# Third cross attention: the exponentials of two key chunks are added on GpSimd before the denominators are summed on TensorE

## The chip, the cores and the metric

One core of a Trainium2 chip runs the whole program in one launch. The metric is the device time of one execution in microseconds (us). The time of a kernel is the median of several executions.

## The reference, cut to what matters

The program is eight layers on x of shape (8, 128, 256): four pairs of a gated cross attention and a gated feed-forward layer. The change is in the third cross attention (L2). With x normalised as the query and the context as key and value, both (batch, 128, 256) read as D = 128 by T = 256:

```python
qh = q.reshape(B, 8, 16, 256)          # 8 heads of 16 rows, 256 queries
kh, vh = k.reshape(B, 8, 16, 256), v.reshape(B, 8, 16, 256)
qn, kn = _l2norm(qh, axis=-2), _l2norm(kh, axis=-2)
sm = softmax(5.0 * einsum('bhdq,bhdk->bhqk', qn, kn), axis=-1)
out = einsum('bhqk,bhdk->bhdq', sm, vh)
x = x + tanh(g_xattn[2]) * out
```

The softmax is computed as exponentials of the scores (no maximum is taken off, since they lie within 5), a product of the exponentials with the values, a sum of the exponentials over the 256 keys (the denominator), and a division at the end.

## The kernel before, in words

The program is written for each engine by hand: each engine has one queue in which its instructions stand in order, and waits on semaphores order them against other engines. The layers run one after another. In this layer (`xa2_*`) the names are these:

- A **step** u = 0 to 15 is one batch b = u // 2 and one half k = u % 2 of its heads: four heads, numbered g = 0 to 3. All is f32. The 256 keys come in two **chunks** kc of 128 (DC = 2).
- `scores(u)` (L1392, matmuls at L1403) makes the scores of four heads, transposed: keys on partitions, 256 queries in the free direction. Four heads sit in four row groups of the array (32 rows each). The results are in two pairs of PSUM banks: pair 2u for heads 0 and 1, pair 2u + 1 for heads 2 and 3. It waits for the masked keys (`km_ready`), the normalised query of the batch (`q2_ready`, once per batch) and for a pair of banks to be free (`p2_ready`).
- ScalarE (L1446) exponentiates one pair at a time, 128x1024, into a slot of `PT2`. PT2 has four slots, which is two steps; a slot holds [head of the pair, chunk, query]. It waits for `v2_done` of the step two before.
- `values(u)` (L1408) waits until both pairs are exponentiated. Then for each chunk it has four passes for the values (L1418, one per head, into four column groups of 32, so they run side by side) and four passes with ones as weights (L1422) that sum the exponentials over the keys of that chunk into `total`. Both accumulate in one PSUM bank over chunks and both halves of the heads. The four denominator passes of the last chunk each count up `v2_done`. `values(2b)` waits also for `o2_read`, count b - 1, which VectorE gives when it has divided batch b - 2 (there are two such banks).
- TensorE's order is scores(0), then scores(u + 1), values(u) in turn, and values(15).
- VectorE (`xa2_dve`, L1457) first does for all eight batches: clamp of the query norms (L1345, 128x256 in SBUF, in place), reciprocal (L1347), multiplication of the query by it (L1462, two SBUF operands), which gives `q2_ready`. After the eighth it goes on to `norm_dve` (L293 on): for each batch a reciprocal of `total` (L1468), the product with `out` and the gate (L1470), which gives `o2_read`, the addition to X (L1472, two SBUF operands), and the steps of the next layer norm (L304 statistics, L301, L307 `ve`, and, for the batch two before, L311 that needs the root from GpSimd).
- GpSimd (`xa2_pool`, L1450) first masks the keys of the later four batches (L1365), then has one instruction per batch, the reciprocal root of the variance for the next layer norm (`rstd_pool`, L317), which waits for `ve` from VectorE. 
- SyncE loads weights of the next layers; the load of `w_up` waits for the last batch's addition to X.
- `hT` is a large buffer of the feed-forward layers; its first two of six rows are not used while this attention runs.

Of the kernel before, what the change touches and what calls it, by code (L numbers as in the profile page):

```python
# [12 lines left out]
ALU = mybir.AluOpType  # L13
# [8 lines left out]
NB = 8  # L22
S = 128
D = 256
DC = D // P
# [105 lines left out]
def build(nc, A, out):  # L131
    ctx = ExitStack()
    with ctx:
        sems = {}

        def sig(name):
            if name not in sems:
                sems[name] = ctx.enter_context(nc.semaphore(name))
            return sems[name]

        def sb(name, shape, dt=F32):
            return ctx.enter_context(nc.sbuf_tensor(name, [P] + shape, dt))[...]
# [14 lines left out]
        hT = sb("hT", [6, T])  # L157
# [47 lines left out]
        a = Arena(weights)  # L205
# [5 lines left out]
        a = Arena(arena)  # L211
# [7 lines left out]
        a = Arena(arena)  # L219
# [5 lines left out]
        a = Arena(weights)  # L225
# [4 lines left out]
        a = Arena(arena)  # L230
# [10 lines left out]
        a = Arena(arena)  # L241
# [9 lines left out]
        a = Arena(arena)  # L251
        a.at = 8576
        PT2 = a.tile([4, 2, DC, D])
        sq2, inv2 = a.tile([NB, D]), a.tile([NB, D])
        VP = a.tile([DC, NB, H2, 2 * D2])
        ones2 = a.tile([2, 2 * D2])
        KM = a.tile([NB // 2, 2, D])
        KM_late = sq2.rearrange("p (b k) d -> p b k d", k=2)
        a = Arena(weights)
        gw, gwT = a.tile([D]), a.tile([DC, E2])  # L260
        weights_shared = a.at
# [9 lines left out]
        a = Arena(arena)  # L271
# [6 lines left out]
        a = Arena(arena)  # L278
# [4 lines left out]
        a = Arena(hT.rearrange("p a b -> p (a b)"))  # L283
# [31 lines left out]
        def rstd_pool(pool, l, t):  # L315
            pool.wait_ge(sig("ln_var"), NB * l + t + 1)
            pool.tensor_tensor(rstd[:, t:t + 1], ve[:, t:t + 1], neg_half[:, t:t + 1], ALU.pow).then_inc(sig("ln_rstd"), 1)  # L317
# [998 lines left out]
        STEPS2 = NB * 2  # L1316
        PAIRS2, SLOTS2 = 3, 4

        def pair_banks(p):

            return 2 * (p % PAIRS2)

        def out2_bank(b):

            bank = psum[:, 6 + (b + ids["out2_first"]) % 2, :]
            return bank[:, 0:D], bank[:, D:2 * D]

        def norms_pe(pe, which, squares):

            for i in range(4):  # L1330
                pe.wait_ge(sig(which + "_squares"), i + 1)
                bank = ring_a.claim(pe)
                ids[which, i] = ring_a.fill(pe.matmul(bank, blk16.rearrange("p a b -> p (a b)"),
                                                      squares[:, 2 * i:2 * i + 2, :].rearrange("p a b -> p (a b)"),
                                                      start=True, stop=True))
# [24 lines left out]
        def keys_of_pair(b):  # L1360
            return KM[:, b, :, :] if b < NB // 2 else KM_late[:, b - NB // 2, :, :]

        def masked_keys(pool, b):

            pool.tensor_tensor(keys_of_pair(b), bc(cx[:, b, :].unsqueeze(1), [P, 2, D]),  # L1365
                               bc(par.unsqueeze(2), [P, 2, D]), ALU.mult).then_inc(sig("km_ready"), 1)
# [18 lines left out]
        def xa2_pe(pe):  # L1385
            norms_pe(pe, "q2", sq2)
            pe.wait_ge(sig("vp_ready"), N_VP)
            pe.wait_ge(ring_a.evacuated, ids["q2", 3])
            pe.wait_ge(ring_v.evacuated, ring_v.filled)
            ids["out2_first"] = ring_v.filled % 2  # L1390

            def scores(u):  # L1392
                b, k = divmod(u, 2)
                if k == 0:
                    pe.wait_ge(sig("km_ready"), b + 1)
                    pe.wait_ge(sig("q2_ready"), b + 1)
                if 2 * u + 1 >= PAIRS2:
                    pe.wait_ge(sig("p2_ready"), 2 * u + 2 - PAIRS2)
                for kc in range(DC):
                    for g in range(4):  # L1400
                        rows = slice(32 * g, 32 * g + 32)
                        bank = psum[:, pair_banks(2 * u + g // 2) + g % 2, :]
                        mm = pe.matmul(bank[:, kc * D:(kc + 1) * D], keys_of_pair(b)[rows, k, kc * P:(kc + 1) * P],  # L1403
                                       xn[rows, b, :], start=True, stop=True)
                        if kc == DC - 1:
                            mm.then_inc(sig(f"s2_pair{g // 2}_full"), 1)

            def values(u):  # L1408
                b, k = divmod(u, 2)
                out, total = out2_bank(b)  # L1410
                if k == 0 and b >= 2:
                    pe.wait_ge(sig("o2_read"), b - 1)
                pe.wait_ge(sig("p2_ready"), 2 * u + 2)
                for kc in range(DC):
                    first, last = k == 0 and kc == 0, k == 1 and kc == DC - 1
                    for g in range(4):
                        p = PT2[:, (2 * u + g // 2) % SLOTS2, g % 2, kc, :]
                        pe.matmul(out[32 * g:32 * g + 32, :], VP[:, kc, b, 2 * g + k, :], p,  # L1418
                                  start=first, stop=last, skip_group_check=True)
                    for g in range(4):  # L1420
                        p = PT2[:, (2 * u + g // 2) % SLOTS2, g % 2, kc, :]
                        mm = pe.matmul(total[32 * g:32 * g + 32, :], ones2[:, k, :], p,  # L1422
                                       start=False, stop=last, skip_group_check=True)
                        if kc == DC - 1:
                            mm.then_inc(sig("v2_done"), 1)

            for u in range(STEPS2 + 1):
                if u < STEPS2:
                    scores(u)
                if u >= 1:  # L1430
                    values(u - 1)
            pe.wait_ge(sig("o2_read"), NB - 1)
# [17 lines left out]
        def xa2_pool(pool):  # L1450
            pool.wait_ge(ring_a.full, ids["q2", 3])
            for b in range(NB // 2, NB):
                masked_keys(pool, b)
            for b in range(NB):
                rstd_pool(pool, 5, b)

        def xa2_dve(dve, step):  # L1457
# [680 lines left out]
        @block.gpsimd  # L2138
        def _(pool):
            consts_pool(pool)  # L2140
            for l, f in list(enumerate([xa0_pool, keys2_pool, xa1_pool, values2_pool, xa2_pool, ff2_pool, xa3_pool, ff3_pool])):
                if l != 5:
                    layernorm_pool(pool, l)
                if f is not None:
                    f(pool)
# [28 lines left out]
```

## Time and profile before

| | us |
|---|---|
| median of the runs (3) | 1039.25 |
| lowest and highest | 1035.27, 1040.14 |
| the profiled execution | 1044.17 |
| its span, first to last instruction | 1042.3 |

| engine | busy in the span, us | share |
|---|---|---|
| TensorE (PE) | 917.7 | 88% |
| VectorE (DVE) | 714.0 | 69% |
| ScalarE (ACT) | 460.9 | 44% |
| GpSimd (POOL) | 343.2 | 33% |

The profile comes from one execution, so its durations add up to that execution's time and not to the median. The stage of the change lies from about 634 to 690 us of the span. A row of the timeline gives start, duration, engine, line, operation, the tile written and read, their shapes, and how many instructions are merged (x8); in brackets stands for how long the engine was idle before it and what ended that. A matmul at f32 has two records, so eight records of L1418 are one group of four heads. Rows of neighbouring groups overlap a little, so the pace is read from one start to the next. Names like PE psum L1422 as a releaser mean the instruction of that engine and line that gave the last missing signal.

### The profile page before, as it was taken

The page shows a single profiled execution, that of the slowest core. Times are in us where ns is not written, and L with a number is a line of the kernel's source. Part 1 is how long each engine was busy: PE and PEld are TensorE (multiplying, and loading weights), DVE is VectorE, ACT ScalarE, POOL GpSimd, SP SyncE. Part 2 cuts the span into 40 slices and gives each one's busy share as a digit, 9 for nine tenths or more (in the row PEclk, how much of TensorE's full clock was granted, in tenths as well). Part 3 has the DMA queues.
Part 4 walks back from the last instruction along what each step waited for, and adds up shares of the span by engine and source line. Part 5 has one row for each costly group of instructions (what it writes and reads, how often), then busy time and mean ns, then how long its engine had stood idle before and what let it go on. Part 6 is the DMA issues. An engine that isn't in the chain of part 4 may idle for free.

```text
span 1042.3 us, 18549 instructions
## 1 busy us (share of the span) xinstructions
PE 917.7 (88%) x6466; PEld 566.1 (54%) x6466; DVE 714.0 (69%) x1490; ACT 460.9 (44%) x747; POOL 343.2 (33%) x365
## 2 busy tenths in 40 slices
PE   7799889999996787778777898989899799989997
PEld 4466665444655454444445454564796466844443
DVE  4978772544499999999996978644112501399998
ACT  3343323110048999999996345631133246210000
POOL 4243121010146566666663712004104537310002
PEclk9988898999998899999998998979899899699999
DMA  9200002000000000000000005246314225000001
GB/s 287 29 1 1 1 22 75 1 0 1 0 1 1 2 2 0 0 0 0 0 0 29 1 1 142 74 127 150 118 51 136 66 70 153 1 0 0 0 0 40
DMA packets 54275, 41.28 MB, mean 40 GB/s; under 512 B 17569, under 2 KB 52028, under 8 KB 54220
## 3 DMA queue, kind: packets, MB, share of 16 engines
q1 hardware_dynamic: 52684, 36.36, 12.6%
q0 software_dynamic: 1536, 4.20, 1.2%
q8 instruction: 34, 0.56, 0.2%
q14 instruction: 21, 0.17, 0.1%
HBM read 33.20 MB, written 7.34 MB: 39 GB/s over the span
## 4 chain that ended last, share of the span: by engine, by line
PE 60%; DVE 23%; issue 9%; ACT 4%; DVEq 2%; another core or an unknown queue 1%; DMA 1%; POOL 1%; SPq 0%; ACTq 0%; POOLq 0%
PE psum L443 6%; PE psum L950 6%; PE psum L941 5%; DVE xn L2032 4%; PE psum L480 3%; PE psum L1531 3%; PE psum L593 2%; PE psum L609 2%; PE psum L956 2%; PE psum L447 2%; PE psum L1221 2%; DVE am L1103 2%; PE psum L1974 2%; PE psum L1813 2%; PE psum L1774 2%
## 5 line engine op out<-in xcount | busy, mean ns | idle before, releaser
L1041 POOL TENSOR_SCALAR arena<-arena 128x1024 f16<-128x1024 f32 x128 | 134.0, 1047 | 95.5 <-ACT arena L1015 92.5
L1103 DVE TENSOR_REDUCE am<-psum 128x1024 f32 (+1 forms) x128 | 154.9, 1212 | 8.7 <-PE psum L941 8.6
L1015 ACT ACTIVATE arena<-psum,am 128x1024 f32<-128x1024 f32 x128 | 143.0, 1125 | 10.3 <-DVE am L1103 8.2
L950 PE MATMUL psum<-identh,arena 128*128 128x128 f16 x1024 | 81.9, 225 | 37.2 <-DVE xn L1108 36.3
L950 PEld LDWEIGHTS psum<-identh,arena 128*128 128x128 f16 x1024 | 63.0, 100 | 94.3 <-issue 61.5
L1974 PE MATMUL psum<-arena,cT 128*128 x512 | 110.9, 379 | 3.3 <-DVE xn L2032 2.8
L317 POOL TENSOR_TENSOR rstd<-ve,neg_half 128x1 f32<-128x1 f32 x64 | 39.3, 619 | 221.1 <-DVE ve L307 220.8
L2032 DVE SCALAR_TENSOR_TENSOR xn<-psum,small,xn 128x256 f32<-128x256 f32 x248 | 102.2, 477 | 4.9 <-DVE xn L2032 2.2
L941 PE MATMUL psum<-arena 96*128 96x512 bf16 x256 | 78.9, 392 | 11.6 <-ACT arena L1015 8.8
L1974 PEld LDWEIGHTS psum<-arena,cT 128*128 128x128 f16 x512 | 50.0, 98 | 63.8 <-DVE xn L2032 4.0
L1008 ACT ACTIVATE arena<-psum,m 128x1024 bf16<-128x1024 f16 x64 | 71.7, 1120 | 2.4 <-PE psum L950 2.4
L660 POOL TENSOR_TENSOR arena<-arena,mask 128x1024 f32<-128x1024 f32 x16 | 30.2, 1910 | 59.6 <-PE psum L593 59.6
L1885 POOL TENSOR_TENSOR hT<-hT,weights 128x512 f16<-128x512 f32 x32 | 39.6, 1268 | 26.4 <-PE psum L1732 26.4
L956 PE MATMUL psum<-arena 128*128 128x16 bf16 x1024 | 45.9, 171 | 1.1 <-ACT arena L1008 1.0
L443 PE MATMUL psum<-xT,arena 128*128 128x512 f32 (+1 forms) x96 | 45.2, 593 | 0.0
L645 ACT ACTIVATE arena<-arena 128x512 f32<-128x512 f32 x32 | 20.1, 629 | 55.9 <-DVE arena L699 55.9
L1114 DVE TENSOR_SCALAR arena<-psum 128x1024 bf16<-128x1024 f16 x64 | 43.7, 683 | 0.0
L467 DVE TENSOR_TENSOR hT<-psum,sg 128x512 f32<-128x512 f32 (+2 forms) x18 | 12.4, 690 | 45.1 <-PE psum L447 35.8
L2049 POOL TENSOR_TENSOR xn<-xn,weights 128x256 f32<-128x256 f32 x4 | 2.9, 731 | 115.0 <-DVE xn L2032 115.0
L459 ACT ACTIVATE sg<-psum 128x512 f32<-128x512 f32 (+2 forms) x18 | 10.7, 596 | 67.6 <-PE psum L447 51.0
L956 PEld LDWEIGHTS psum<-arena 128*128 128x128 bf16 x1024 | 36.4, 97 | 7.6 <-ACT arena L1008 1.5
L593 PE MATMUL psum<-arena 128*128 128x512 f32 x64 | 39.6, 707 | 0.8 <-ACT arena L627 0.8
(341 smaller groups left out, 1856.4 us busy)
## 6 DMA issues: line engine op xcount, KB each, us to landing
hT<-in_L_ffn_expert_masks SPq DMA_DIRECT2D x32, 256.0 KB, 2.8
arena<-in_L_ffn_w_gate SPq DMA_DIRECT2D x2, 1408.0 KB
arena<-in_L_ffn_w_up SPq DMA_DIRECT2D x2, 1408.0 KB
arena<-in_L_ffn_w_down SPq DMA_DIRECT2D x2, 1408.0 KB
moe_in<-xT SPq DMA_DIRECT2D x2, 1024.0 KB, 6.8
hT<-moe_in SPq DMA_DIRECT2D x4, 512.0 KB, 5.2
moe_out<-arena SPq DMA_DIRECT2D x16, 128.0 KB, 1.7
weights<-in_L_ffn_w SPq DMA_DIRECT2D x2, 640.0 KB, 6.8
```

What stands on the lines that cost most here:

```text
L443: mm = pe.matmul(bank[0:fn, :], w[:, c, f0:f0 + fn], xT[:, c, g * HALF:(g + 1) * HALF], start=(c == 0), stop=(c == DC - 1 and lora is None))
L593: ids["s0", n] = ring_v.fill(pe.matmul(bank, qT0[:, i // 2, b * S:(b + 1) * S], kBD0[:, b % 2, i // 2, 4 * (i % 2):4 * (i % 2) + 4, :].rea ...
L941: mm = pe.matmul(psum[:, 2 * SCORES[h] + g, :], QT[0:SPLIT, h, bass.ds(i * P, P)], KT[0:SPLIT, h, g * HALF:(g + 1) * HALF], start=True, st ...
L950: mm = pe.transpose(bank[:, k * P:(k + 1) * P], Y1[:, hm % 2, k * P:(k + 1) * P], identh)
L956: mm = pe.matmul(psum[:, SCORE_BANKS + hm % TB, 0:HD], PT1[:, hm % 2, k, :], V1[:, k, hm * HD:(hm + 1) * HD], start=(k == 0), stop=(k == N ...
L1008: act.activation(PT1[:, hm % 2, :, :], psum[:, SCORE_BANKS + hm % TB, :].bitcast(FP16), ACT.Identity, bias=m1024).then_inc(sig("pt1_by_act ...
L1015: act.activation(PE1[:, h % 2, :], scores, ACT.Exp, bias=am[:, bass.ds(n, 1)], accum_out=qs[:, bass.ds(n, 1)]).then_inc(sig("p1_ready"), 1)
L1041: pool.tensor_scalar(Y1[:, n % 2, :], PE1[:, n % 2, :], 255.0, 1024.0, ALU.mult, ALU.add)\
L1103: dve.tensor_reduce(am[:, bass.ds(n, 1)], psum[:, 2 * SCORES[h]:2 * SCORES[h] + 2, :], AX.XY, ALU.max, negate=True)\
L1114: dve.tensor_scalar(PT1[:, hm % 2, :, :], psum[:, SCORE_BANKS + hm % TB, :].bitcast(FP16), 1024.0, None, ALU.subtract).then_inc(sig("pt1_b ...
L1974: mm = pe.matmul(bank, x[:, c, t * P:(t + 1) * P], WTp[:, bass.ds(ep, 1), :, c, :], start=(i == 0 and c == 0), stop=(i == 1 and c == DC - 1))
L2032: r = dve.scalar_tensor_tensor(acc, y, hot3p[:, t, bass.ds(ep, 1), k], acc, ALU.mult, ALU.add)
```

## The change

A tile PS2 is laid over the first two rows of hT: [two halves by step parity, four heads, 256 queries]. In `values(u)` the denominator passes are taken out of the loop over chunks. Behind the loop TensorE waits for `sum2_ready` and then makes four passes over PS2, once per step. On GpSimd, each step has two additions of 128x512 f32, one per pair: chunk 0 plus chunk 1. Each waits for the exponentials of its pair and, from step 2 on, for `v2_done` of the step two before. The roots `rstd_pool(5, b)` for b = 0 to 4 now stand behind the additions of the steps 6, 8, 10, 12 and 14, and those for b = 5 to 7 behind the last addition.

```diff
@@ -256,6 +256,7 @@
         KM_late = sq2.rearrange("p (b k) d -> p b k d", k=2)
+        PS2 = hT[:, 0:2, :].rearrange("p a n -> p (a n)").rearrange("p (s g q) -> p s g q", s=2, g=4)
         a = Arena(weights)
@@ -1417,12 +1418,10 @@
                         p = PT2[:, (2 * u + g // 2) % SLOTS2, g % 2, kc, :]
                         pe.matmul(out[32 * g:32 * g + 32, :], VP[:, kc, b, 2 * g + k, :], p,
                                   start=first, stop=last, skip_group_check=True)
-                    for g in range(4):
-                        p = PT2[:, (2 * u + g // 2) % SLOTS2, g % 2, kc, :]
-                        mm = pe.matmul(total[32 * g:32 * g + 32, :], ones2[:, k, :], p,
-                                       start=False, stop=last, skip_group_check=True)
-                        if kc == DC - 1:
-                            mm.then_inc(sig("v2_done"), 1)
+                pe.wait_ge(sig("sum2_ready"), 2 * u + 2)
+                for g in range(4):
+                    pe.matmul(total[32 * g:32 * g + 32, :], ones2[:, k, :], PS2[:, u % 2, g, :],
+                              start=False, stop=(k == 1), skip_group_check=True).then_inc(sig("v2_done"), 1)
 
@@ -1451,7 +1450,17 @@
             for b in range(NB // 2, NB):
                 masked_keys(pool, b)
-            for b in range(NB):
+            for u in range(STEPS2):
+                for i in range(2):
+                    p = PT2[:, (2 * u + i) % SLOTS2, :, :, :]
+                    pool.wait_ge(sig("p2_ready"), 2 * u + i + 1)
+                    if u >= 2:
+                        pool.wait_ge(sig("v2_done"), 4 * (u - 1))
+                    pool.tensor_tensor(PS2[:, u % 2, 2 * i:2 * i + 2, :], p[:, :, 0, :], p[:, :, 1, :], ALU.add)\
+                        .then_inc(sig("sum2_ready"), 1)
+                if u >= 6 and u % 2 == 0:
+                    rstd_pool(pool, 5, (u - 6) // 2)
+            for b in range((STEPS2 - 6) // 2, NB):
                 rstd_pool(pool, 5, b)
```

## Rows read from the trace of the kernel before

**Rows 1.** Timeline, 634 to 655 us: start, duration, engine, line, operation, [idle before <- releaser]

```profile
634.32 0.43 DVE L1462 TENSOR_TENSOR xn<-xn,arena 128x256 f32<-128x256 f32 x1
634.66 1.13 DVE L1345 TENSOR_SCALAR arena<-arena 128x256 f32<-128x256 f32 x1
...
635.83 1.75 DVE L1347 RECIPROCAL arena<-arena 128x256 f32<-128x256 f32 x1
...
640.06 0.42 DVE L1462 TENSOR_TENSOR xn<-xn,arena 128x256 f32<-128x256 f32 x1
...
640.40 0.29 DVE L1345 TENSOR_SCALAR arena<-arena 128x256 f32<-128x256 f32 x1
...
652.32 0.43 DVE L1462 TENSOR_TENSOR xn<-xn,arena 128x256 f32<-128x256 f32 x1
...
654.45 0.48 DVE L1470 SCALAR_TENSOR_TENSOR arena<-psum,gates,arena 128x256 f32<-128x256 f32 x1
...
654.98 0.64 PE L1418 MATMUL psum<-arena 128*32 128x256 f32 x8 [1.34 <-DVE arena L1470]
```

**Rows 2.** Timeline, a step of the middle, and a division after it

```profile
659.79 1.15 PE L1403 MATMUL psum<-xn,arena 32*128 32x256 f32 x16
...
660.86 0.64 PE L1418 MATMUL psum<-arena 128*32 128x256 f32 x8
660.99 1.94 ACT L1446 ACTIVATE arena<-psum 128x1024 f32<-128x1024 f32 x2 [1.00 <-PE psum L1403]
...
661.32 0.61 PE L1422 MATMUL psum<-arena 128*32 128x256 f32 x8
...
661.75 0.61 PE L1418 MATMUL psum<-arena 128*32 128x256 f32 x8
...
662.73 1.15 PE L1403 MATMUL psum<-xn,arena 32*128 32x256 f32 x16
...
665.88 1.76 DVE L1468 RECIPROCAL arena<-psum 128x256 f32<-128x256 f32 x1 [2.31 <-PE psum L1422]
```

**Rows 3.** Waits, 634 to 692 us: who waited for whom, total us, times, longest

```profile
POOL rstd L317 <- DVE ve L307: 52.5, 7, 23.4
```

**Rows 4.** Timeline, the last division, right behind the last pass

```profile
688.58 1.76 DVE L1468 RECIPROCAL arena<-psum 128x256 f32<-128x256 f32 x1 [1.49 <-PE psum L1422]
```

**Rows 5.** GpSimd's groups by form: count | busy us, mean ns | idle before

```profile
L1885 POOL TENSOR_TENSOR hT<-hT,weights 128x512 f16<-128x512 f32 x32 | 39.6, 1268 | 26.4 <-PE psum L1732 26.4
L317 POOL TENSOR_TENSOR rstd<-ve,neg_half 128x1 f32<-128x1 f32 x64 | 39.3, 619 | 221.1 <-DVE ve L307 220.8
...
L1358 POOL TENSOR_TENSOR cx<-cx,arena 128x512 f32<-128x512 f32 x4 | 5.1, 1269 | 65.8 <-DVE arena L1347 65.8
...
L1354 POOL TENSOR_TENSOR arena<-cx 128x512 f32<-128x512 f32 x4 | 4.1, 1047 | 0.0
```

**Rows 6.** GpSimd's L1365: all eight (min/median/max ns); the one at 634.4; timeline from 631.3

```profile
L1365 POOL TENSOR_TENSOR arena<-cx,par x8: 1034/1382/2416, 589.3 to 634.4; 128x512 f32<-128x512 f32 x8
...
L1365 POOL TENSOR_TENSOR arena<-cx,par x1: 1287/1287/1287, 634.4 to 634.4; 128x512 f32<-128x512 f32 x1
...
631.31 4.33 POOL L1365 TENSOR_TENSOR arena<-cx,par 128x512 f32<-128x512 f32 x4 [2.37 <-PE psum L1333]
...
632.53 1.75 DVE L1347 RECIPROCAL arena<-arena 128x256 f32<-128x256 f32 x1
```

**Rows 7.** Busy time in two stretches, and TensorE's granted clock (PEclk)

```profile
634.80:644.00 9.20, 8.00 (x68) 4.23 (x72) 8.96 (x11) 3.88 (x4) 0.84 (x1) 0.51 0.23 53
658.00:688.00 30.00, 29.81 (x492) 16.73 (x496) 18.48 (x40) 19.38 (x20) 3.79 (x6) 1.00 0.01 2
```

**Rows 8.** Timeline, TensorE at the start of the stage

```profile
634.89 2.09 PE L1403 MATMUL psum<-xn,arena 32*128 32x256 f32 x16 [3.67 <-DVE xn L1462]
...
638.09 2.09 PE L1403 MATMUL psum<-xn,arena 32*128 32x256 f32 x16 [1.11 <-ACT arena L1446]
...
640.11 1.08 PE L1418 MATMUL psum<-arena 128*32 128x256 f32 x8
...
643.68 1.15 PE L1403 MATMUL psum<-xn,arena 32*128 32x256 f32 x16
```

## The prediction, written before the changed kernel was run

> **What bounds the kernel now.** I read the stage in four steps: the timeline of its start (the chain that ended last runs through the same instructions), one step in its middle, the list of waits, and its end. From 634.9 to 655.0 us TensorE is not the limit. VectorE clamps, inverts and multiplies the norms of the eight batches one after another, with no gap: a multiplication (L1462) starts every 2.45 us (640.06 to 652.32 are five periods), and only behind the last does the same queue come to the first division (L1468, then L1470 at 654.45). TensorE's `values(4)` needs that division (o2_read), sits idle 1.34 us for it and starts at 654.98 [rows 1]. Whatever lengthens VectorE's chain before that moment moves the end one for one, and what TensorE saves before it is lost in a longer wait.
>
> From 654.98 on TensorE is the limit. A step is 2.94 us (L1403 at 659.79 and at 662.73): scores 1.07, then four groups of passes at about 0.43, of which two are the denominators of L1422. ScalarE's two exponentials take 1.94 and it waits 1.00 us in each step [rows 2], and GpSimd has nothing but a reciprocal root per batch [rows 3]. The last pass ends right before 688.58, where VectorE takes over with the last division [rows 4]. So the new work is put on an engine that is free, but it comes between two that are not.
>
> **What it removes.** One group of L1422 per step, 16 in all. Each is 0.43 us (661.32 to 661.75) [rows 2]. The four of steps 0 to 3 lie before the wait at 654.98 and bring nothing. Twelve lie behind it: 12 x 0.43 = 5.2 us. This is the most that can be gained, and it comes only if nothing else is later than TensorE.
>
> **What it adds on GpSimd.** 32 additions of 128x512 f32. No such addition is in the trace; its neighbours of the same size fall into two kinds. The product of two different full tensors takes 1.27 us (L1358; L1885, with an f16 result, 1268 ns). With the same tensor twice (L1354) it is 1.05, and as fast with broadcast operands (L1365 at its quickest, 1034) [rows 5, 6]. The new addition reads two different halves of PT2, so I take 1.27 and keep 1.04 as the low end. The high end is 1.4, for the two-piece access pattern. Between neighbouring instructions lie some 0.04 us (four of L1365 in 4.33 us, against their own durations) [rows 6], so an addition holds GpSimd for 1.31. [...] With the fast kind the sum below would be 5.5 us less.
>
> **Behind TensorE's wait.** Two additions are 2.63 us per step, every second step also has a `rstd_pool`, 0.62 on average and 0.65 with its gap [rows 5]: 5.9 us for two steps, where TensorE takes 5.88 now and would take 5.02. So GpSimd becomes the limit, just at the old pace. From `values(4)` on: the additions of step 6 can start when its scores are exponentiated, 0.89 + 0.43 + 0.12 + 1.07 + 1.02 = 3.5 us later (two groups of values, one of denominators, the seam between steps, scores, one exponential) (steps 4 and 5 are added before). Then 20 x 1.31 + 5 x 0.65 = 29.5, then the last four passes and their end, 0.5, and some 0.2 of handing over: 33.7, against 688.58 - 654.98 = 33.6 now. The gain of 5.2 is gone and the change here is +0.1. With 1.04 GpSimd would need 4 x 1.08 + 0.65 = 5.0 per batch and nearly all of the gain would stay. In TensorE's queue the next scores and values stand behind the new wait; ScalarE has its exponentials ready a step ahead, so it isn't next.
>
> **Before `values(4)`: the port.** This is the largest term. The trace shows what happens when the two engines work on SBUF at once. At 634.32 VectorE multiplies two SBUF tensors (0.43); GpSimd's product that starts at 634.4 takes 1287 ns instead of 1034. VectorE's clamp then starts at 634.66 and takes 1.13 us, where it takes 0.29 later: it ends when GpSimd's product does. The reciprocal takes 1.75 us at 632.53, with GpSimd busy, and at 635.83, without it [rows 1, 6]. So whoever comes second waits for the whole instruction, for the clamp and the multiplication, not for the reciprocal. The Trainium skill, SBUF — State Buffer, section "Who interferes with whom", says so too: an exclusive lock for the whole instruction, for a VectorE instruction with two SBUF inputs or in a two-port mode. With the row's 0.85 us for each meeting, and six to twelve meetings, the term would be 5.1 to 10.2; with the rule, by which each waits for what is left of the other, it is the 7.9 of the walk below.
>
> In the kernel before GpSimd has finished at 635.7, so just one batch pays. Afterwards it has the 12 additions of steps 0 to 5 in this stretch: their exponentials end between 638 and 656. I walked the six later multiplications with that rule (the arrival order decides; additions 1.27 long with 0.04 between them). An addition that still runs when the reciprocal ends delays the multiplication; one that queued meanwhile goes next, and the clamp waits for all of it. The multiplications end before at 640.5, 642.9, 645.4, 647.8, 650.3 and 652.7, and in the walk at 641.2, 644.4, 647.9, 652.4, 656.9 and 660.6. That is +7.9 us for the first division. Bounds: 12 additions are 15.8 us of GpSimd. If each blocked VectorE from end to end it would be 15.8, and if seven reciprocals (12.3) hid as many as fit, 3.5. With additions of 1.04 the walk gives 4.9.
>
> **The clock.** TensorE then has nothing to do for some 9 us ahead of `values(4)`. The rows show what such a pause did: idle before 634.89 for 3.67 us, the granted clock 0.51 of full speed over 634.8 to 644.0, which is the level of 1.2 GHz, four groups in 643.68 - 640.11 = 3.57 us (0.89 each), and full speed from 643.68 on, 8.8 us after it resumed [rows 7, 8]. The same for 8.8 us behind `values(4)`: a step at the half level was 643.68 - 638.09 = 5.6 us and is 4.7 without one group, 1.75 more than GpSimd's 2.95, and 1.87 such steps fit: +3.3. Low end 0 (the clock holds, as it did from 658 to 688 [rows 7]), high end 6.
>
> **What costs nothing.** The addition to X (L1472) also has two SBUF inputs and will wait for up to one addition per batch. VectorE idles 2.31 us ahead of a division (665.88 [rows 2]), so it needs 3.6 of the 5.9 of a batch: hidden, and out of hiding only above 2.3 us a batch. The roots are moved behind the additions of step 2b + 6; VectorE asks for root b after division b + 2, which is about a step later in the walk: hidden. `v2_done` still comes from four passes, and ScalarE's wait on it is for two steps back. No transfer is moved except with the end of the stage: w_up is loaded when the last division is done. The tail of divisions, roots and transposes behind 688.58 is the same.
>
> **Sum.** +7.9 (VectorE's chain) + 0.1 (GpSimd in place of TensorE) + 3.3 (clock) = +11.3 us. On the profiled execution's own 1044.17 us that is 1055.5; that execution lies 4.9 above the median of the runs, 1039.25, so on the median it is 1050.5, which I forecast.
>
> **The rivals.**
> 1. Fast additions (1.04), the port as read: +4.9 - 2.5 = +2.4, with the clock's 3.3 up to +5.7: 1041.7 to 1045, middle 1043.5. For it: L1354 and L1365. Against: every product here of two different f32 tensors is slow. 0.15.
> 2. The port costs nothing, because additions happen to fall into the reciprocals; they still take 1.27: `values(4)` stays at 655, +0.1 and no pause: 1039.5. Against: rows 6, and two additions per exponential pair are longer than a reciprocal. 0.13.
> 3. Faster: TensorE stays the limit behind 654.98. It needs both, additions below (5.02 - 0.65)/4 = 1.09 us with their gap, and a free port. Then up to 12 x 0.43 come through, less 0.3 to 1.3 in the last step, where the final passes wait for additions that nothing covers: -3.9 to -5.2, 1035. For it: rows 3 show GpSimd empty, and its fast kind is just under that bound. 0.06.
> 4. Worse: the clock stays at its half level for longer than once, since TensorE now pauses in each step, or the additions take 1.4 (walk +9.1, then +2.9 and the clock's 3.3): +15 to +18: 1056. 0.14.
> The forecast has 0.52.
>
> **How the numbers follow.** Range: rival 3 and the far half of 4 are left out, 0.06 + 0.07, and what lies at the edges: 1037 to 1057. Half a per cent is 5.2 us, about what can be told from no change here. Slower by more than that (above 1044.4): the forecast, 4 and a little under half of 1: 0.73. Within: rival 2 and most of 1: 0.20. Faster: rival 3: 0.07.
>
> **What would show it.** Duration of the new GpSimd instruction: 1.27 or 1.04. L1345 and L1462 between 638 and 661: durations of 1 us and more, where they are 0.29 and 0.42, show the port; all at the old values show rival 2. The wait of `values(4)` for L1470 grows from 1.3 to some 9 us, and the granted clock is half for some us behind it. In the steady stretch the idle time before the denominators is ended by GpSimd and a batch takes about 5.9 us; 5.1 would show rival 3. Wrong would be the sum above all if VectorE wins the port whenever it asks, or if the clock holds through the pause.

## The result, and the profile after

| | before | after |
|---|---|---|
| median, us (6 runs each) | 1036.09 | 1045.41 |
| lowest and highest | 1033.57, 1040.14 | 1045.0, 1047.09 |
| profiled execution, its span | 1044.17, 1042.3 | 1045.38, 1043.3 |

The ratio after to before is 1.0087, 95% interval 1.0063 to 1.0110: 9 us slower (6.5 to 11.4). Forecast were +11.3 us and slower by more than 0.5%. The profiled execution of the kernel before was a long one of its kind, so the two spans lie only 1 us apart, and the stage has to be compared by itself. Part of that length can be seen: some 120 us behind the stage TensorE waits 7.08 us for ScalarE, and 0.56 us in the trace after. Before and after:

```profile
815.81 6.37 PE L1774 MATMUL psum<-small,arena 128*128 128x512 f32 x8 [7.08 <-ACT vaug L1854]
```

```profile
819.00 3.70 PE L1783 MATMUL psum<-small,arena 128*128 128x512 f32 x8 [0.56 <-ACT vaug L1863]
```

I measure the stage in each trace from the start of the first multiplication of the queries (634.32 in [rows 1], L1471 after) to the start of the last division (688.58 in [rows 4], L1477 after). One line of busy times for each kernel gives that stretch and the rest behind it; the columns are TensorE, its weight loads, VectorE, ScalarE, GpSimd, granted clock, DMA share, GB/s. Before:

```profile
634.32:688.58 54.26, 51.06 (x770) 28.26 (x770) 41.54 (x67) 31.42 (x33) 5.11 (x8) 0.91 0.27 70
688.58:1042.30 353.72, 324.67 (x1706) 209.47 (x1704) 184.45 (x486) 78.31 (x145) 87.69 (x90) 0.93 0.23 67
```

After:

```profile
637.48:698.25 60.77, 47.92 (x642) 23.84 (x642) 53.55 (x68) 31.43 (x33) 46.30 (x40) 0.87 0.25 63
698.25:1043.30 345.05, 324.47 (x1706) 209.63 (x1704) 184.38 (x486) 78.64 (x145) 87.49 (x90) 0.93 0.24 69
```

The stage went from 54.26 to 60.77 us, +6.5. TensorE is busy 3.1 us less in it, GpSimd 41 us more, and VectorE 12 us more although it has the same 67 or 68 instructions: some of them take longer, which is a wait inside the instruction. The timeline after, from the first additions (L1459) to `values(4)` (L1419):

```profile
641.27 2.55 POOL L1459 TENSOR_TENSOR hT<-arena 128x512 f32<-128x512 f32 x2 [2.47 <-ACT arena L1445]
...
643.22 0.88 DVE L1471 TENSOR_TENSOR xn<-xn,arena 128x256 f32<-128x256 f32 x1
...
648.62 5.33 POOL L1459 TENSOR_TENSOR hT<-arena 128x512 f32<-128x512 f32 x4 [1.57 <-ACT arena L1445]
...
650.12 1.41 DVE L1346 TENSOR_SCALAR arena<-arena 128x256 f32<-128x256 f32 x1
...
657.06 1.39 DVE L1346 TENSOR_SCALAR arena<-arena 128x256 f32<-128x256 f32 x1
...
660.61 1.75 DVE L1477 RECIPROCAL arena<-psum 128x256 f32<-128x256 f32 x1
...
662.94 1.94 PE L1419 MATMUL psum<-arena 128*32 128x256 f32 x16 [7.22 <-DVE arena L1479]
```

This answers to [rows 1]. Two additions take 2.55 us. While they run, multiplications take 0.88 in place of 0.42 and two clamps 1.4 in place of 0.28. Over the eight batches five multiplications lose 2.6 us together and two clamps 2.2. That is 4.8, and by just that the first division is late (23.13 us behind the first multiplication, 18.34 before). TensorE waits 7.22 us for it where it waited 1.34. The reciprocals of the queries between them remain at 1.75.

The granted clock in four stretches after (as in [rows 7]):

```profile
637.00:647.20 10.20, 8.04 (x72) 4.48 (x72) 9.96 (x11) 4.76 (x5) 6.90 (x6) 0.53 0.31 83
648.00:660.00 12.00, 7.25 (x115) 3.58 (x104) 11.79 (x10) 7.28 (x8) 10.60 (x8) 1.00 0.93 235
660.00:667.50 7.50, 4.56 (x44) 2.27 (x48) 6.74 (x12) 0.00 (x0) 0.00 (x0) 0.54 0.11 34
668.00:698.00 30.00, 26.51 (x404) 12.56 (x396) 24.74 (x35) 18.98 (x20) 29.28 (x26) 1.00 0.01 2
```

In the pause the clock falls to its half level, and it is back 4.2 us after TensorE resumed at 662.94:

```profile
666.80:667.00 0.20, 0.20 (x8) 0.20 (x4) 0.15 (x2) 0.00 (x0) 0.00 (x0) 0.50 0.00 0
667.20:667.40 0.20, 0.20 (x8) 0.00 (x0) 0.00 (x0) 0.00 (x0) 0.00 (x0) 1.00 0.00 0
```

From 668 on GpSimd is busy 29.28 of 30 us: it is the limit. Two steps of the steady stretch, to be held against [rows 2]:

```profile
676.81 0.58 POOL L318 TENSOR_TENSOR rstd<-ve,neg_half 128x1 f32<-128x1 f32 x1
...
677.32 5.31 POOL L1459 TENSOR_TENSOR hT<-arena 128x512 f32<-128x512 f32 x4
677.50 1.40 DVE L1481 TENSOR_TENSOR X<-X,arena 128x256 f32<-128x256 f32 x1
...
680.13 0.64 PE L1423 MATMUL psum<-hT,arena 128*32 128x256 f32 x8 [0.47 <-POOL hT L1459]
...
682.60 0.54 POOL L318 TENSOR_TENSOR rstd<-ve,neg_half 128x1 f32<-128x1 f32 x1
```

A batch takes 682.60 - 676.81 = 5.79 us, against 5.88 before, and TensorE waits ahead of the denominators for the additions.

### The profile page after: what moved, and what is told of

It reads as the page before. It is cut to its first block, busy times and chain, and to the rows that moved or that the text cites. A ratio compares the mean times of both kernels' runs of the same rounds, so it can differ in the third digit from the quotient of the medians.

```text
span 1043.3 us, 18353 instructions
## 1 busy us (share of the span) xinstructions
PE 918.7 (88%) x6338; PEld 563.5 (54%) x6338; DVE 724.8 (69%) x1490; ACT 460.9 (44%) x747; POOL 383.9 (37%) x397
## 3 DMA queue, kind: packets, MB, share of 16 engines
q1 hardware_dynamic: 52684, 36.36, 12.5%
## 4 chain that ended last, share of the span: by engine, by line
PE 60%; DVE 20%; issue 9%; ACT 4%; POOL 3%; DVEq 2%; DMA 1%; SPq 0%; ACTq 0%; POOLq 0%
PE psum L444 6%; PE psum L951 6%; PE psum L942 5%; DVE xn L2041 4%; PE psum L481 3%; PE psum L1540 3%; PE psum L594 3%; PE psum L610 2%; PE psum L1222 2%; PE psum L957 2%; POOL hT L1459 2%; PE psum L424 2%; PE psum L448 2%; DVE am L1104 2%; PE psum L1983 2%
## 5 line engine op out<-in xcount | busy, mean ns | idle before, releaser
L1459 POOL TENSOR_TENSOR hT<-arena 128x512 f32<-128x512 f32 x32 | 42.1, 1344 | 14.2 <-ACT arena L1445 14.2
L1445 ACT ACTIVATE arena<-psum 128x1024 f32<-128x1024 f32 x32 | 31.0, 1021 | 26.3 <-PE psum L1404 26.3
```

What stands on the lines that cost most here:

```text
L1459: pool.tensor_tensor(PS2[:, u % 2, 2 * i:2 * i + 2, :], p[:, :, 0, :], p[:, :, 1, :], ALU.add)\
```

## The experiments

Each was compared with the kernel before on the same chip; the groups e1 to e4, e5 to e8, e9 to e11 and e12 ran on four different chips. "Stage" is the stretch defined above, "first division" the start of it behind the first multiplication, both from the trace; "behind" is from the end of the product that frees `values(4)` to the last division.

| kernel | first division | behind | stage | ratio to before (95%) |
|---|---|---|---|---|
| before | 18.34 | 33.65 | 54.26 | |
| after | 23.13 | 35.37 | 60.77 | 1.0087 (1.0063 to 1.0110) |
| after, again (e5) | 23.22 | 35.50 | 60.98 | 1.0094 (1.0064 to 1.0124) |
| late additions only (e1) | 18.33 | 34.03 | 54.63 | 0.9986 (0.9954 to 1.0018) |
| early additions only (e2) | 23.21 | 34.86 | 60.33 | 1.0068 (1.0041 to 1.0095) |
| pause kept busy (e3) | 23.22 | 33.40 | 58.89 | 0.9966 (0.9936 to 0.9996) |
| the same again (e6) | 23.23 | 33.44 | 58.93 | 1.0022 (0.9985 to 1.0060) |
| memsets for early additions (e4) | 20.74 | 35.00 | 58.00 | 1.0005 (0.9974 to 1.0037) |
| fast additions (e9) | 21.04 | 31.33 | 54.63 | 1.0011 (0.9984 to 1.0037) |
| VectorE reordered, no additions (e7) | 13.43 | 37.13 | 52.82 | 0.9942 (0.9913 to 0.9972) |
| the same again (e12) | 13.44 | 37.19 | 52.89 | 0.9951 (0.9918 to 0.9984) |
| reordered, ten steps added (e8) | 14.41 | 39.18 | 55.85 | 1.0023 (0.9996 to 1.0049) |
| reordered, five steps added (e10) | 13.43 | 35.83 | 51.53 | 0.9972 (0.9947 to 0.9997) |
| before, delayed (e11) | 18.34 | 35.11 | 55.72 | 0.9994 (0.9970 to 1.0018) |

The stages of repeated kernels agree within 0.2 us. The ratios are not as sharp: half an interval is 3 to 4 us.

**Which half of the additions costs.** The theory: in the early steps VectorE's instructions wait for GpSimd's at the SBUF port that they share, and then the clock is low. The rival: TensorE's new wait in the steady steps. Both kernels keep the two groups of L1422 in the steps that are not added:

```diff
+        SUMMED = list(range(6, STEPS2))     # e1; list(range(6)) in e2
+                    if u not in SUMMED:
+                        for g in range(4):
+                            p = PT2[:, (2 * u + g // 2) % SLOTS2, g % 2, kc, :]
+                            mm = pe.matmul(total[32 * g:32 * g + 32, :], ones2[:, k, :], p,
+                                           start=False, stop=last, skip_group_check=True)
...
-                for i in range(2):
+                for i in range(2 if u in SUMMED else 0):
```

> Additions on GpSimd only for the steps 6 to 15; the steps 0 to 5 sum both chunks on TensorE as before. Theory (port, then clock): the first division and values(4) are where they were in the kernel before (20.7 us after the first multiplication of the queries starts, against 25.5 in the changed kernel), there is no long pause and no half clock behind it, and from values(4) to the last division it takes 33.2 to 34 us, since GpSimd needs as long per batch as TensorE did. Time against the kernel before: -1 to +1 us. Rival (TensorE's waits for the additions in the steady steps are what costs): still +4 to +9 us.

> Additions on GpSimd only for the steps 0 to 5, the later ones as before. Theory (port, then clock): values(4) is late by 4.8 us as in the changed kernel, the clock is at half for some us behind it, and since TensorE is the limit again behind it that costs it 2 to 3 us: +6.5 to +8 us against the kernel before. Rival (waits in the steady steps): -1 to +0.5 us.

e1: stage 54.63, ratio 0.9986. e2: stage 60.33, ratio 1.0068. So the early additions alone bring 6.1 of the 6.5 us, and 20 of the 32 additions, the ones behind the pause, cost 0.4 and gain nothing. The wait of `values(4)` for the division, in e1 (1.37 us, as before) and in e2:

```profile
663.46 0.64 PE L1420 MATMUL psum<-arena 128*32 128x256 f32 x8 [1.37 <-DVE arena L1488]
```

```profile
659.72 1.94 PE L1420 MATMUL psum<-arena 128*32 128x256 f32 x16 [7.21 <-DVE arena L1488]
```

The rival falls. Behind the pause e2 needs 34.86 in place of 33.65, less than the 2 to 3 us expected for the clock.

**What in the early additions holds VectorE.** In e4 GpSimd is as long busy and gives the same signals, but reads nothing (PS2 is filled with ones once, ahead of the steps; the early denominators are then wrong):

```diff
+                    if u < 6:
+                        if 2 * u + i:
+                            pool.wait_ge(sig("sum2_ready"), 2 * u + i)
+                        pool.memset(BUSY2, 1.0).then_inc(sig("sum2_ready"), 1)
```

> Changed kernel, but for the steps 0 to 5 GpSimd fills an unused stretch of 128x1472 f32 (a memset, some 1.3 us, reads nothing from SBUF) in place of each addition; the denominators of these steps are thereby sums of ones and the output differs. Theory (the read side of the port is what VectorE's multiplication waits for): L1471's rows are back at 0.42 us, and the clamps L1346 wait at most as in the changed kernel (two waits of 1.1): first division 0 to 2.2 us late in place of 4.8, and the total +0 to +4 us against the kernel before. Rival (GpSimd's being busy or its signals delay VectorE, whatever it does): the same 4.8 late and +9.

A multiplication and the clamp behind it on VectorE in e4, and the memsets of GpSimd at that time:

```profile
651.68 0.42 DVE L1478 TENSOR_TENSOR xn<-xn,arena 128x256 f32<-128x256 f32 x1
652.03 0.78 DVE L1347 TENSOR_SCALAR arena<-arena 128x256 f32<-128x256 f32 x1
```

```profile
645.46 11.61 POOL L1464 MEMSET hT<- 128x1472 f32 x8 [1.46 <-ACT arena L1446]
```

All eight multiplications are at 0.42 with GpSimd busy from 645.46 to 657.07. Only the clamps wait, five of them by 0.3 to 0.7 us, and the first division is 2.4 us late, a little above the 0 to 2.2 expected. So it is the additions' reading that the multiplication waits for, and the clamp waits for a GpSimd instruction that only writes, too. The Trainium skill, SBUF — State Buffer, section "Who interferes with whom", has both: two SBUF inputs contend only with a GpSimd instruction that reads, a two-port instruction, which a `tensor_scalar` like the clamp can be, with any. The trace agrees, with 0.42 against 0.88 for the first and 0.28 against 0.78 for the second.

**The clock.** e3 puts matmuls whose result nobody reads into the pause:

```diff
+                if u == 4:
+                    pe.wait_ge(sig("p2_ready"), 10)
+                    for i in range(14):
+                        mm = pe.matmul(psum[:, pair_banks(12), 0:D], identf, xn[:, 0, :], start=True, stop=True)
+                    mm.then_inc(sig("pause_filled"), 1)
+                    pe.wait_ge(sig("pause_filled"), 1)
```

> The changed kernel, with 14 matmuls of 128x256 f32 (some 6 us at the full level) whose result nobody reads, put between scores(5) and values(4), to keep TensorE busy in the pause. Theory of the clock term: values(4) stays late by 4.8 us, but the granted clock stays at 1.0 behind it, and the stretch to the last division shrinks from 35.3 to 33.2 to 33.8 us: 1.5 to 2.5 us faster than the changed kernel, +6.5 to +8 against the kernel before. Rival (the clock costs nothing, since GpSimd sets the pace there anyway): as slow as the changed kernel, +9.

> The kernel with the 14 idle matmuls in the pause once more. First run: the stage 1.9 us shorter than in the changed kernel, as expected, but the whole execution some 7 to 10 us shorter, with a mean granted clock of 0.947 against some 0.935, the difference lying in later layers. If that belongs to the kernel (what TensorE did in the pause has a hold on when the clock falls later), the mean clock is again at or above 0.943 and the time again below that of the kernel before. If it was the chip or the hour, the stage is again 58.9 us and the time +4 to +8 us against the kernel before.

The same stretch as above, 660.0 to 667.5, in e3:

```profile
660.00:667.50 7.50, 6.46 (x99) 3.43 (x97) 7.11 (x12) 2.77 (x3) 2.24 (x2) 1.00 0.01 2
```

The clock is at its full level, `values(4)` is as late as in the kernel after (23.22 to the first division), and behind it the stage takes 33.40 in place of 35.37: the fallen clock was worth 2.0 us, and without it the steady part is 0.2 us shorter than before. That much came as expected, twice. The whole time did not. The ratio was 0.9966 in e3 and 1.0022 in e6, 12.5 and 7.5 us below the kernel after, of which the stage explains 1.9. e6 came between the two outcomes that were expected of it: its mean clock was high again (0.943), but its time was not below that of the kernel before (-1.6 to +6.2 us), and its middle, +2.3, does not reach the +4 to +8 of the other. In the traces most of the difference lies behind the stage, in layers whose instructions are the same. Both traces from there on:

```profile
694.82:1032.30 337.48, 316.00 (x1706) 201.50 (x1704) 184.33 (x486) 78.32 (x145) 87.60 (x90) 0.96 0.24 71
```

```profile
695.52:1033.00 337.48, 315.93 (x1706) 201.40 (x1704) 184.39 (x486) 78.27 (x145) 87.58 (x90) 0.96 0.25 71
```

337.48 us twice at a clock of 0.96, where the kernel after has 345.05 at 0.93, and 344.91 in its repetition:

> The changed kernel once more, on the same chip and in the same rounds as the other kernels of this group. From the first multiplication of the queries to the last division some 60.8 us again, against 54.3 before; time +6.5 to +9.5 us against the kernel before. If the layers behind the stage are slower in this kernel in general, its mean granted clock is lower than that of the kernel before in most executions; if not, the means are alike but for the half clock of the pause (about 0.003).

The stage of e5 is 60.98, its ratio 1.0094. The clock averaged over whole executions differs too: 0.931 (e5), 0.937 (kernel before on the same chip), 0.943 (e6). The pause was to account for 0.003 of it, so these means speak for a lower clock of the kernel after outside its pause too; with six executions of e5 between 0.925 and 0.937 they don't prove it.

The traces show where the time behind the stage goes. These are the same 10 us, counted from 190 us behind the last division, in the kernel after and in e3:

```profile
888.25:898.25 10.00, 10.00 (x64) 10.00 (x64) 1.96 (x8) 2.42 (x3) 4.68 (x4) 0.54 0.00 1
```

```profile
884.82:894.82 10.00, 8.70 (x88) 8.39 (x88) 2.84 (x10) 5.87 (x8) 5.10 (x5) 1.00 0.01 2
```

In the kernel after the clock falls there although TensorE has had no gap (busy 20.00 of the 20 us before, 868.25 to 888.25), and sixteen records of the same matmul (L1822) take 3.58 us in place of 1.93. In e5 it falls at the same place (0.54), in e3 and e6 it doesn't. But it falls there in e1 too (0.51), a kernel whose time is that of the kernel before, and the executions of e6 go from 1032 to 1047 us, at mean clocks of 0.951 to 0.933. One trace shows one execution; how often the clock falls in which kernel isn't shown by them.

**Is it the moment at which the stage ends?** e11 is the kernel before with six of those matmuls ahead of the wait.

> The kernel before, with six matmuls whose result nobody reads put ahead of the wait of values(4), 2.6 us of which 1.3 are the wait that is there anyway: the stage is 1.3 us longer (55.6 in place of 54.3), and nothing else differs. Theory (the granted clock in later layers depends on the moment at which the stage ends and on nothing in its work, so a pure delay changes it too): the time from the last division to the end is 336 to 339 us in the trace, as with the idle matmuls in the changed kernel, and the median time differs from the kernel before by something else than +1.3, most likely -3 to -7 us. Rival (later layers don't care): +1.3 us.

The stage is 1.46 us longer as planned, and the ratio is 0.9994 (0.9970 to 1.0018): -3.1 to +1.9 us, which holds the +1.3 of the rival and hardly the -3 to -7 of the theory. The theory that the moment alone decides is not borne out; other delays were not tried. The trace has 352.3 us behind the stage, but this is no test of the 336 to 339 expected. In e9, e10 and e11, all on a chip where the kernel before took 1046.6 us against 1036 to 1040 elsewhere, and in the trace of the kernel before, TensorE waits 7.1 to 7.2 us for ScalarE's L1854 (or its line there) as shown under the result; in the ten other traces it is 0.56. These four are the ones with 352 us and more behind the stage. Why ScalarE is late there is not shown.

**The speed of an addition.** e9 adds chunk 0 to itself.

```diff
-pool.tensor_tensor(PS2[:, u % 2, 2 * i:2 * i + 2, :], p[:, :, 0, :], p[:, :, 1, :], ALU.add)
+pool.tensor_tensor(PS2[:, u % 2, 2 * i:2 * i + 2, :], p[:, :, 0, :], p[:, :, 0, :], ALU.add)
```

> The changed kernel with the same half of PT2 as both operands of each addition (chunk 0 twice), so the denominators are not the reference's. Theory (two different full tensors are the slow kind of product or sum on GpSimd, the same tensor twice the fast one): the addition takes 1.04 us in place of 1.27, values(4) is late by 2 to 4 us in place of 4.8, and behind it a batch takes 5.0 to 5.3 us in place of 5.8, so the stage is 55 to 58 us (changed kernel 60.8, before 54.3). Rival (the access pattern makes it slow, not the second tensor): still 1.27 and 60.8.

GpSimd's additions in the kernel after and in e9, with the durations in ns as min/median/max:

```profile
L1459 POOL TENSOR_TENSOR hT<-arena x32: 1281/1304/1512, 641.3 to 695.9; 128x512 f32<-128x512 f32 x32
```

```profile
L1459 POOL TENSOR_TENSOR hT<-arena x32: 1039/1040/1222, 636.5 to 685.3; 128x512 f32<-128x512 f32 x32
```

The access pattern is the same; only the second tensor differs. An addition of two different tensors is slow, of a tensor with itself fast. The shorter one takes both terms down: the first division is 2.7 us late in place of 4.8, and a batch in the steady part is 5.16 us (roots at 668.23 and 673.39). The stage is 54.63, just above the one before and below the 55 to 58 expected, and the ratio 1.0011: even at that speed the change gains nothing.

**Is there a version that gains?** Since `values(4)` waits for VectorE's chain, e7 leaves TensorE and GpSimd alone and moves two norms behind divisions:

```diff
-            for b in range(NB):
+            for b in range(6):
+                query(b)                    # clamp, reciprocal, multiplication as before
...
+                if b < 2:                   # at the end of add(b), the division of batch b
+                    query(b + 6)
```

> The kernel before (no addition on GpSimd), with VectorE's queue reordered: norms of batches 0 to 5, division of batch 0, norm of 6, division of 1, norm of 7, and on. Theory (values(4) waits for VectorE's chain): the wait of 1.3 us at values(4) is gone, stage 54.3 - 1.3 = 53.0 us, -1 to -1.5 us. Rival (another engine is as late): stage 54.0 or more, no change.

> The reordered kernel without additions on GpSimd once more. Its stage was 1.4 us shorter, as expected, but its median 6 us below the kernel before, with a mean granted clock of 0.946 against 0.937. If that is the kernel's own, again -4 to -7 us and a higher clock than the kernel before; if it was the chip or the hour, the stage is again 52.8 us and the time -0.5 to -3 us.

The stage is 52.82 and 52.89, 1.4 us shorter, as expected. By the ratios (0.9942 and 0.9951) the time is 6.0 and 5.1 us shorter: again more than the stage gives, on two occasions, with a mean clock of 0.946 and 0.944 against 0.937 and 0.936 for the kernel before beside them. In the trace of e12:

```profile
636.64:689.53 52.89, 51.03 (x770) 28.32 (x770) 41.28 (x67) 31.42 (x33) 5.10 (x8) 0.91 0.28 72
689.53:1027.50 337.97, 314.39 (x1706) 200.86 (x1704) 184.33 (x486) 78.21 (x145) 87.49 (x90) 0.97 0.24 70
```

There is no fall of the clock 190 us behind the stage in this trace either. Executions of e7 go from 1025 to 1039 us at mean clocks of 0.954 to 0.933, so one and the same kernel runs at both levels. What decides between them stayed open.

With this order additions can be put where VectorE has slack. e8 adds in ten steps, e10 in the steps 6, 8, 10, 12 and 14.

> VectorE's queue as in the reordered kernel, and additions on GpSimd in ten of the sixteen steps (2, 3, 4, 6, 7, 8, 10, 11, 12, 14), the others with both denominator passes on TensorE. Theory: GpSimd needs about 9.2 us for four steps and TensorE 10.5, so TensorE stays the limit and the port's waits fall on a chain that has slack: 1.3 + 10 x 0.43 = 5.6 us at most, 4 to 5.6 less in the stage (48.7 to 50.3 us) and in the time. Rival (the port holds VectorE so much that its divisions are late again): stage 52 us or more, gain under 2.5.

> VectorE's queue reordered as in the kernel that was faster (norms of 0 to 5, division of 0, norm of 6, division of 1, norm of 7), and additions on GpSimd only in the steps 6, 8, 10, 12 and 14, each followed by a step without, so that an addition has a full step more until TensorE asks for it. Theory: no wait for GpSimd, 5 x 0.43 = 2.1 us less than the 52.8 of the reordered kernel: stage 50.5 to 51.3 us, some 3.3 us less than before; the whole time -3 us, give or take 4 for the clock in later layers. Rival (the port's waits for the divisions and the root behind the additions eat it): stage 52.5 or more.

e8 missed: stage 55.85, 3 us above the order alone. Its trace shows two causes. VectorE has norms and divisions to do at the same time and its clamps again take 1.4; and GpSimd's queue:

```profile
666.66 0.55 POOL L318 TENSOR_TENSOR rstd<-ve,neg_half 128x1 f32<-128x1 f32 x1 [2.94 <-DVE ve L308]
667.18 5.28 POOL L1468 TENSOR_TENSOR hT<-arena 128x512 f32<-128x512 f32 x4
668.28 0.48 DVE L1491 SCALAR_TENSOR_TENSOR arena<-psum,gates,arena 128x256 f32<-128x256 f32 x1
668.80 1.19 DVE L1493 TENSOR_TENSOR X<-X,arena 128x256 f32<-128x256 f32 x1
669.76 0.64 PE L1432 MATMUL psum<-hT,arena 128*32 128x256 f32 x8 [3.27 <-POOL hT L1468]
```

The first root waits 2.94 us for VectorE's variance, the additions of step 7 stand behind it, and TensorE waits 3.27 us for them. e10 has no addition behind a waiting root. Its stage is 51.53, 1.3 less than the order alone, where five groups would be 2.1, and so just outside the 50.5 to 51.3 expected. The ratio is 0.9972 (0.9947 to 0.9997). It beats the kernel before by its stage, 2.7 us; that it beats e7, measured on other chips, is shown for the stage alone.

## Why the prediction was right, point by point

**What bounds the stage.** The traces bear it out. In e1 the wait of `values(4)` is where it was; in e7, where the division is moved ahead, 1.4 us come free.

**Removed passes.** The 5.2 us were to be gained only if TensorE stayed the limit. It did not: it is busy 3.1 us less in the stage and that shows nowhere.

**The addition, 1.27 us.** Measured 1.28 for pairs without a meeting (2.55 for two), median 1304 ns. The choice by "two different tensors" was right, and e9 shows it by itself. The high end of 1.4 was only reached where VectorE came first (up to 1512 ns). The gap of 0.04 us between neighbours was misread: in [rows 6] the four durations add up to more than their 4.33 us, and after, two records of 1303 and 1294 ns take 2.55 us, so the records overlap. The 1.31 per addition came nevertheless (5.28 us for four, 677.32 to 682.60), because meetings with VectorE lengthen some of them; that the two errors cancel is luck.

**GpSimd in place of TensorE, +0.1.** Right in mechanism and size: with the clock kept up (e3) -0.2 us, and a batch 5.79 against the 5.9 worked out.

**VectorE's chain, +7.9.** The mechanism was right, the size was not: 4.8. The walk let six multiplications and the clamps behind them meet additions; in the trace five multiplications wait, mostly 0.46 us, and only two clamps. A clamp waits only if an addition is queued at that very moment, and GpSimd, waiting for the next exponentials, often had none. The rule behind the walk held: all five multiplications end 0.27 to 0.29 us behind the addition that was running when they started. What failed was the timing: the walk let too many clamps find an addition queued. The bound from below, 3.5, was nearer than the walk.

**The clock, +3.3.** Right in kind, too large: 2.0 by e3, since it was back 4.2 us after TensorE resumed and not 8.8 (with 4.2 the prediction's own sum gives 1.6). In the stretch 648 to 660 after, most of the pause included, it is still 1.00: it fell late in the pause.

**What was put at nothing.** L1481 waits for the port in the steady part (1.00 to 2.73 in place of 0.42) and stays hidden behind TensorE. The prediction had it wait for one addition at most; the longest wait covers two, one running and one queued (it ends 0.3 us behind the second of the four):

```profile
688.88 5.32 POOL L1459 TENSOR_TENSOR hT<-arena 128x512 f32<-128x512 f32 x4
689.00 2.73 DVE L1481 TENSOR_TENSOR X<-X,arena 128x256 f32<-128x256 f32 x1
```

Hidden is also L312, the normalisation, which I had not counted: 0.41 in the tail, where GpSimd adds nothing (701.42), and in the kernel after, with an addition running,

```profile
672.26 0.92 DVE L312 TENSOR_SCALAR xn<-X,mv,rstd 128x256 f32<-128x256 f32 x1
```

The roots are in time.

**The sum** was 11.3 for the stage and 6.5 came. The whole time rose by 9 all the same, by which the forecast looks better than it was, and that is luck: some 3 us of it don't lie in the stage, and the prediction had everything outside it at nothing. The stage alone (6.5 and 6.7) lies at the lower edge of both measured intervals, so the surplus is likely, from them and from the mean clocks, but its size and its cause are not shown.

**Rivals.** Rival 1 (fast additions) is answered for its own case by e9: its -2.5 behind the wait came (-2.3), its +4.9 ahead of it was 2.7, so the stage was +0.4 where +2.4 was worked out without the clock. Rival 2 needed additions to fall into the reciprocals, rival 3 a free port: neither happened. Rival 4 put the clock down for longer; it was down for less.

## What to carry to other kernels

Work that is moved to a free engine has to be checked for the port and the queue it shares with the engines that aren't free: here 12 additions on an idle GpSimd delayed a chain on VectorE by 4.8 us, and that chain was the one the stage waited for. Moved work gains only if the engine that takes it needs less time per round than the engine it relieves: four additions of 1.3 us and a root took GpSimd 5.79 us per batch, and TensorE had needed 5.88 for everything. Ask first what the waiting engine waits for: moving two norms in VectorE's queue, with no work taken away, made the stage 1.4 us shorter.

## What was not expected of the hardware

- GpSimd's addition of 128x512 f32 takes 1.04 us with one tensor as both operands and 1.28 to 1.30 with two different ones.
- An f32 `tensor_scalar` with two scalars per partition (L312) is held up by additions too (0.92 in place of 0.41), although at 0.41 it is no faster than a multiplication of two tensors.
- A GpSimd memset holds up VectorE's clamp (0.78 in place of 0.28) but not its multiplication of two SBUF tensors (0.42).
- VectorE's addition to X (two SBUF inputs) once waited for two of GpSimd's additions in a row (2.73 us), the second of which had only been queued when it started.
- The granted clock can fall while TensorE is busy without a gap: 0.54 over 888.25 to 898.25 after, with TensorE busy 20.00 of the 20 us before. The time behind the stage, with the same instructions, was 337.5 us in two traces of one kernel, without this fall, and 345 in two of another, with it. Over whole executions the kernels' mean clocks ranged from 0.931 to 0.947. A change of the stage by 1.4 us (e7, e12) came with 5 to 6 us of the whole time, twice. A pure delay of 1.5 us (e11) did not do it. How the clock of later layers hangs on the earlier ones, if it does, is open.
